# Expert masks of the second token half made inside the FFN block loop, mask and logit copies on ScalarE, and one silu moved ahead of the weight rows

## The chip, the cores and the metric

The kernel runs on one core of one Trainium2 chip. The metric is the device time of one execution in microseconds, the median of the runs. Names used below: TensorE is PE (PEld is its weight load), VectorE is DVE, ScalarE is ACT, GpSimd is POOL, SyncE is SP.

## The reference

Input x has 1024 tokens of 256 features. Four residual stages follow, each with a layer norm in front: attention (16 query heads, 4 key heads, sink and window mask), an FFN with a LoRA mixture of experts, a state-space mixer, and the same FFN with the same weights again. The change touches the FFN only, so it acts twice.

```python
def _L0_ffn_ref(x, gate_w, w_up, w_gate, w_down, up_A, up_B, gate_A, gate_B, down_A, down_B):
    gate_logits = jnp.einsum('bsd,ed->bse', x, gate_w)
    topw, sel = jax.lax.top_k(gate_logits, TOP_K)
    topw = jax.nn.softmax(topw.astype(jnp.float32), axis=1).astype(x.dtype)
    ...
    base_up = xt @ w_up.T
    base_gate = xt @ w_gate.T
    for e in range(NUM_EXPERTS):
        c = jnp.sum(jnp.where(sf == e, wf, 0.0), axis=1)
        lo_up = LORA_ALPHA * (xt @ up_A[e].T @ up_B[e].T)
        lo_gate = LORA_ALPHA * (xt @ gate_A[e].T @ gate_B[e].T)
        h_e = jax.nn.silu(base_up + lo_up) * (base_gate + lo_gate)
        ch = c[:, None] * h_e
        mixed_h = mixed_h + ch
        lora_down = lora_down + LORA_ALPHA * (ch @ down_A[e].T @ down_B[e].T)
    out = mixed_h @ w_down.T + lora_down
```

There are 8 experts of rank 16, so all ranks together are 128 rows. Each token has its top 2 experts. The softmax runs over the tokens (axis 1), so its maximum and sum need the logits of all 1024 tokens.

## The kernel before

All of it is one program written out by hand: for each engine a Python function issues the instructions in the order in which the engine runs them, and semaphores join the engines. `need(e, name, n)` is a wait until counter `name` has reached n. No scheduler moves anything. Float32 products are made of three matmuls of high and low parts (`three`, L167), so most of PE's rows have line 167.

**The FFN** (`ffn`) works on two halves of 512 tokens and on six blocks (`HB`) of 128 hidden features. A unit i = 6h + b is half h, block b, and N = 12. Block 5 holds only 64 features, and its up and gate parts are packed in one bank. The two expert choices of a token are slots 0 and 1. Per unit:

- `base_x(i)`: x times the up and gate weights, 6 matmuls of 512 columns into each of two PSUM banks, `2*which + i % 2` (banks 0 and 2, or 1 and 3). A packed block uses bank `i % 2` alone.
- `base_lora(i)`: adds slot 0's LoRA part from `f_um` (6 matmuls). ScalarE then takes `silu(i, 0)`, and DVE multiplies by the gate, `gated(i, 0)`, which writes `f_t`.
- `second(i)`: adds slot 1's difference to the same banks (6 matmuls), then `silu(i, 1)` and `gated(i, 1)`. It waits for `gated(i, 0)` (counter t0).
- `ch` = `f_t` times the weight row `f_wb`, `mixed` adds both slots, and `hi_parts` (ACT) and `lo_parts` (DVE) split the results in high and low parts. `down(i)` multiplies them (6 matmuls of 512 and 12 of 256 columns).

PE's loop step i runs `base_x(i)`, `base_lora(i)`, `second(i-1)`, `down(i-2)`. `base_x(i)` waits for counter t1 to reach i-1, that is for `gated(i-2, 1)`, which frees the banks. DVE's step i runs `slot(i, 0)` (gated and ch), then `slot(i-1, 1)`, `mixed(i-1)`, `lo_parts(i-1)`. ACT's step i runs `silu(i, 0)`, `silu(i-1, 1)`, `hi_parts(i-1)`.

**Masks.** For each half, `top` finds the best logits of a token, `top_index` their expert numbers, and `one_hot` (L1146) turns these into 0/1 rows `f_hot`. `masks(h)` (L914) transposes them on PE into banks 4 and 5. ACT copies slot 0's mask (`mask0`, L1054), and DVE copies slot 1's and takes the difference (`mask1`, L1160 and L1161). `masked` (L1180) multiplies the LoRA activations `f_us` by the masks in 8 instructions, which write `f_um`. `base_lora` of block 0 waits for the first four of them, `second` for all eight.

**Before the loop** stands the preparation: the layer norm of half 1 (`norm` on DVE, transposes L235 on PE, `hi` on ACT, `lo` L249 on DVE), `logits(1)`, masks of half 0, the softmax's maximum (L975, L978) and sum (L981), `lora_a(1)`, the first units, and `weigh(0)` (L964), which spreads the softmax weights over 128 rows. ACT copies these rows (`weights_out`, L1086). Half 0's layer norm, logits, `lora_a` and `base_x(0)` are issued at the end of the stage in front (`early`). In the first FFN ACT and DVE also split the FFN's weights there (`w_hi` L830, `w_lo` L834). Half 1's index and one-hot rows are made just before and in step 0, its masks in step 2 of PE's loop, and its eight masked products in steps 3 to 5 of DVE's.

## Time and profile before

| | |
|---|---|
| median of 3 runs | 574.26 us (574.2 to 577.9) |
| the profiled execution's own time | 574.69 us |
| its span in the trace | 572.9 us |
| granted TensorE clock | 0.995 |
| PE, DVE, ACT, POOL busy | 523.3, 410.5, 304.3, 131.5 us |

All times of rows are microseconds from the start of the span. The first FFN's preparation lies at 221 to 248 us and its loop from 248 us on; the second FFN's at 445 to 469 us and from 469 us on. A row's idle time and releaser stand in brackets at its end. Rows of several instructions give the time from the first one's start to the last one's end.

### The profile page before, as it was taken

The page shows a single profiled execution, that of the slowest core. Times are in us where ns is not written, and L with a number is a line of the kernel's source. Part 1 is how long each engine was busy: PE and PEld are TensorE (multiplying, and loading weights), DVE is VectorE, ACT ScalarE, POOL GpSimd, SP SyncE. Part 2 cuts the span into 40 slices and gives each one's busy share as a digit, 9 for nine tenths or more (in the row PEclk, how much of TensorE's full clock was granted, in tenths as well). Part 3 has the DMA queues.
Part 4 walks back from the last instruction along what each step waited for, and adds up shares of the span by engine and source line. Part 5 has one row for each costly group of instructions (what it writes and reads, how often), then busy time and mean ns, then how long its engine had stood idle before and what let it go on. Part 6 is the DMA issues. An engine that isn't in the chain of part 4 may idle for free.

```text
span 572.9 us, 9040 instructions
## 1 busy us (share of the span) xinstructions
PE 523.3 (91%) x3031; PEld 439.2 (77%) x3033; DVE 410.5 (72%) x894; ACT 304.3 (53%) x752; POOL 131.5 (23%) x274
## 2 busy tenths in 40 slices
PE   1798899999999979889999999999999889999994
PEld 1577699999999967677887887757778668788884
DVE  6734366666666878889968797966886768886674
ACT  3435677787688643363433454888662245343251
POOL 5511152534342320000000003669443000000000
PEclk9999999999999999999999999999999999999998
DMA  7310010000002103000030000000000000000101
GB/s 269 108 66 1 2 38 0 2 1 2 2 2 72 73 1 133 2 1 0 1 128 2 1 1 1 1 2 1 1 1 2 0 1 1 1 2 0 38 0 38
DMA packets 5790, 14.25 MB, mean 25 GB/s; under 512 B 624, under 2 KB 2928, under 8 KB 5744
## 3 DMA queue, kind: packets, MB, share of 16 engines
q1 hardware_dynamic: 5744, 13.66, 6.8%
q8 instruction: 25, 0.41, 0.3%
q14 instruction: 21, 0.17, 0.1%
HBM read 12.61 MB, written 1.05 MB: 24 GB/s over the span
## 4 chain that ended last, share of the span: by engine, by line
PE 66%; DVE 19%; ACT 6%; issue 6%; POOL 1%; DMA 1%; DVEq 0%; SPq 0%; ACTq 0%; POOLq 0%
PE psum L167 55%; PE psum L446 3%; DVE f_t L1170 2%; DVE f_um L1180 2%; DVE xn L227 2%; PE psum L477 1%; DVE ln_stats L207 1%; DVE oT_hl L665 1%; DMA x_resid<-in_x 1%; PE psum L964 1%; DVE x_resid L672 1%; ACT f_sil L1077 1%; DVE xT_hl L249 1%; ACT qT L540 1%; PE psum L1578 1%
## 5 line engine op out<-in xcount | busy, mean ns | idle before, releaser
L167 PE MATMUL psum<-xT_hl,ffn_w_hl 128*128 128x512 f32 x312 | 78.2, 397 | 7.3 <-DVE f_t L1170 7.3
L167 PE MATMUL psum<-f_um,ffn_w_hl 128*128 128x512 f32 x288 | 72.0, 398 | 1.2 <-DVE f_um L1180 1.2
L167 PEld LDWEIGHTS psum<-xT_hl,ffn_w_hl 128*128 128x128 f32 x312 | 56.3, 188 | 19.6 <-issue 8.7
L167 PEld LDWEIGHTS psum<-f_um,ffn_w_hl 128*128 128x128 f32 x288 | 53.5, 188 | 14.2 <-DVE f_um L1180 2.1
L1170 DVE TENSOR_TENSOR f_t<-psum,f_sil 128x512 f32<-128x512 f32 (+1 forms) x48 | 33.1, 690 | 32.8 <-ACT f_sil L1077 32.2
L1077 ACT ACTIVATE f_sil<-psum 128x512 f32<-128x512 f32 (+1 forms) x48 | 28.2, 595 | 51.9 <-PE psum L167 51.9
L167 PE MATMUL psum<-wo_hl,oT_hl 128*128 128x256 f32 x384 | 50.9, 282 | 4.0 <-DVE oT_hl L665 3.9
L659 DVE TENSOR_TENSOR pT_hl<-psum,pT_hl 126x360 fp32r<-126x360 f32 (+1 forms) x44 | 23.6, 537 | 42.9 <-ACT pT_hl L572 42.9
L167 PE MATMUL psum<-xT_hl,wq_hl 128*128 128x512 f32 x192 | 52.2, 407 | 1.9 <-ACT qT L540 1.9
L167 PEld LDWEIGHTS psum<-wo_hl,oT_hl 128*128 128x128 f32 x384 | 47.7, 188 | 7.5 <-DVE oT_hl L665 5.9
L1098 ACT ACTIVATE f_ch_hl<-f_ch 128x512 fp32r<-128x512 f32 x48 | 30.0, 630 | 41.3 <-DVE f_ch L1227 41.2
L540 ACT ACTIVATE qT<-psum 128x512 f32<-128x512 f32 x32 | 34.9, 1090 | 31.5 <-PE psum L167 31.5
L549 ACT ACTIVATE probs<-probs,small 120x66 f32<-120x66 f32 x120 | 40.5, 344 | 7.8 <-DVE small L642 7.0
L167 PEld LDWEIGHTS psum<-xT_hl,wq_hl 128*128 128x128 f32 x192 | 33.8, 188 | 9.2 <-issue 3.4
L167 PEld LDWEIGHTS psum<-ffn_w_hl,f_mix_hl 128*128 128x128 f32 x288 | 36.9, 188 | 2.8 <-DVE x_resid L1261 0.8
L167 PE MATMUL psum<-f_ch_hl,ffn_w_hl 128*128 128x512 f32 x144 | 37.8, 398 | 1.1 <-DVE f_ch_hl L1239 1.1
L167 PE MATMUL psum<-ffn_w_hl,f_mix_hl 128*128 128x256 f32 x288 | 37.7, 280 | 0.0
L714 POOL TENSOR_TENSOR probs_wide<-probs,small 120x186 f32<-120x186 f32 x40 | 19.9, 498 | 69.7 <-DVE small L622 69.5
L221 POOL TENSOR_TENSOR ln_rstd<-ln_var_eps,minus_half 128x4 f32<-128x4 f32 x8 | 8.3, 1033 | 113.4 <-DVE ln_var_eps L214 113.4
L1227 DVE TENSOR_TENSOR f_ch<-f_t,f_wb 128x512 f32<-128x512 f32 x48 | 33.2, 691 | 1.4
L167 PEld LDWEIGHTS psum<-f_ch_hl,ffn_w_hl 128*128 128x128 f32 x144 | 26.6, 188 | 8.3 <-DVE f_ch_hl L1239 1.7
L167 PE MATMUL psum<-pT_hl,v_hl 126*128 126x360 f32 (+1 forms) x132 | 30.4, 339 | 1.1 <-DVE oT_hl L665 0.6
(238 smaller groups left out, 1129.1 us busy)
## 6 DMA issues: line engine op xcount, KB each, us to landing
w_raw<-in_wq SPq DMA_DIRECT2D x4, 512.0 KB, 3.2
w_raw<-in_wo SPq DMA_DIRECT2D x4, 512.0 KB, 3.3
ffn_w_raw<-in_ffn SPq DMA_DIRECT2D x3, 576.0 KB, 6.1
ffn_w_raw_far<-in_ffn SPq DMA_DIRECT2D x3, 576.0 KB, 6.5
ssd_w_raw<-in_ssd SPq DMA_DIRECT2D x3, 512.0 KB, 5.5
x_resid<-in_x SPq DMA_DIRECT2D x2, 512.0 KB, 4.6
out_x<-x_resid SPq DMA_DIRECT2D x4, 256.0 KB, 2.3
w_raw<-in_wk SPq DMA_DIRECT2D x1, 512.0 KB, 6.7
```

What stands on the lines that cost most here:

```text
L167: i = e.matmul(dst, lhs(a), rhs(b), start=start and n == 0, stop=stop and n == len(TERMS) - 1, **kw)
L227: e.tensor_scalar(xn(t), x[:, t, :], mv[:, t, 0:1], rstd[:, t:t + 1], ALU.subtract, ALU.mult).then_inc(LN["xn"], 1)
L446: m = e.matmul(bank(u % 2)[0:ROWS, i * KBLK:(i + 1) * KBLK], queries_of(q, QB), kw[:, w % W_SLOTS, i, :], start=True, stop=True)
L540: e.activation(qT[:, HALF * half:HALF * half + HALF, h], bank(6), ACT.Copy, scale=float(HD) ** -0.5).then_inc(s_qt, 1)
L549: m = e.activation(p[:, n, :], p[:, n, :], ACT.Exp, bias=NEGM[0:rows, u % 4, n:n + 1], accum_out=DEN[0:rows, u % 4, n:n + 1])
L659: e.tensor_tensor(pT_hl[0:nk, u % 2, LO, 0:n], bank(2 + u % 2)[0:nk, 0:n], f32(pT_hl[0:nk, u % 2, HI, 0:n]), ALU.subtract).then_inc(s_plo, 1)
L714: e.tensor_tensor(wide, p[:, :, SINK:KBLK], spread(r, KB_WIN), ALU.mult)
L1077: e.activation(sil[at_rows, s, :], bank(i % 2)[rows, :], ACT.Silu).then_inc(FS[f"sil{s}"], 1)
L1098: e.activation(ch_hl[:, i % 2, s, HI, :], ch[:, i % 2, s, :], ACT.Copy).then_inc(FS["chh"], 1)
L1170: e.tensor_tensor(tt[rows, s, :], to_bank(i, 1)[rows, :], sil[rows, s, :], ALU.mult).then_inc(FS[f"t{s}"], 1)
L1180: e.tensor_tensor(um_hl[:, h, s, which, w, :], f32(us_hl[:, h, which, w, :]), mT[:, (0, 2)[s], half(h)], ALU.mult).then_inc(FS["um"], 1)
L1227: e.tensor_tensor(ch[:, i % 2, s, :], tt[:, s, :], wb[:, s, half(h)], ALU.mult).then_inc(FS[f"ch{s}"], 1)
```

## The change

- Half 1's masks move from step 2 of PE's loop: slot 0's four transposes stand at the end of step 4 (`MASK_STEP`), slot 1's in step 5 between `base_x(5)` and `base_lora(5)`. Both go to bank 3. Slot 0's wait for t1 = 4, slot 1's for ScalarE's copy of slot 0's mask.
- ScalarE copies all masks out of PSUM (`mask_out`), for half 1 at the end of its step 4, and also the logits of half 1. DVE takes slot 1's difference from the two bf16 copies in SBUF (`mask_diff`).
- On DVE `norm` of half 1 stands ahead of `top_index(0)`. Half 1's `top_index` and `one_hot` move to step 4, its masked products to steps 5 and 6. In half 0 the eighth masked product stands ahead of `gated(0, 0)`.
- On PE the gate part of `base_x(0)` stands behind the transposes of half 1 instead of at the end of the stage in front.
- On ACT `silu(0, 1)` stands ahead of `weights_out(0)`.

```diff
                 else:
                     need(e, "mk0", 1)
-                    need(e, "mk1", 2)
+                    need(e, "mk1", 1)
...
-            def masks(e, h):
-
-                need(e, "ulo", 2 * h + 2)
-                need(e, "hot", 2 * h + 2)
-                for s in range(SLOTS):
-                    for t in range(HT):
-                        m = e.matmul(bank(4 + s)[:, t * P:(t + 1) * P], hot[:, s, HT * h + t, :], identb,
-                                     start=True, stop=True)
-                    m.then_inc(FS["mk"], 1)
+            MASK_BANK = ((4, 5), (3, 3))
+            MASK_STEP = HB - 2
+
+            def masks(e, h, s):
+
+                need(e, "hot", 2 * h + s + 1)
+                if h == 0:
+                    need(e, "ulo", 2)
+                elif s == 0:
+                    need(e, "t1", MASK_STEP)
+                else:
+                    need(e, "mk0", 2)
+                for t in range(HT):
+                    m = e.matmul(bank(MASK_BANK[h][s])[:, t * P:(t + 1) * P], hot[:, s, HT * h + t, :], identb,
+                                 start=True, stop=True)
+                m.then_inc(FS["mk"], 1)
...
                 ln["tr"](e, 1)
+                base_x(e, 0, (1,))
                 base_x(e, 1, (0,))
                 logits(e, 1)
-                masks(e, 0)
+                for s in range(SLOTS):
+                    masks(e, 0, s)
...
                         base_x(e, i)
                         if i == 2:
-                            masks(e, 1)
                             weigh(1)
+                        if i == MASK_STEP + 1:
+                            masks(e, 1, 1)
                         base_lora(e, i)
...
                     if i >= 2:
                         down(i - 2)
+                    if i == MASK_STEP:
+                        masks(e, 1, 0)
...
-                def mask0(h):
-                    need(e, "mk", 2 * h + 1)
-                    e.activation(mT[:, 0, half(h)], bank(4), ACT.Copy).then_inc(FS["mk0"], 1)
+                def mask_out(h):
+                    for s in range(SLOTS):
+                        need(e, "mk", 2 * h + s + 1)
+                        e.activation(mT[:, s, half(h)], bank(MASK_BANK[h][s]), ACT.Copy).then_inc(FS[("mk0", "mk1")[s]], 1)
...
                 ln["hi"](e, 1)
+                need(e, "lg", 2)
+                e.activation(lgT[:, :], bank(6)[0:EXPERTS, :], ACT.Copy).then_inc(FS["lgt"], 1)
                 before["free"](e)
-                mask0(0)
+                mask_out(0)
...
+                silu(0, 1)
                 weights_out(0)
-                silu(0, 1)
...
                         split(4)
-                        mask0(1)
...
                         hi_parts(i - 1)
+                    if i == MASK_STEP:
+                        mask_out(1)
...
-                def mask1(h):
+                def mask_diff(h):
 
                     need(e, "mk0", h + 1)
-                    need(e, "mk", 2 * h + 2)
-                    e.tensor_copy(mT[:, 1, half(h)], bank(5)).then_inc(FS["mk1"], 1)
-                    e.tensor_tensor(mT[:, 2, half(h)], bank(5), mT[:, 0, half(h)], ALU.subtract).then_inc(FS["mk1"], 1)
+                    need(e, "mk1", h + 1)
+                    e.tensor_tensor(mT[:, 2, half(h)], mT[:, 1, half(h)], mT[:, 0, half(h)],
+                                    ALU.subtract).then_inc(FS["mk2"], 1)
...
                 top(e, 0)
+                ln["norm"](e, 1)
                 top_index(e, 0)
-                ln["norm"](e, 1)
...
                 one_hot(0)
-                logits_copy(e, 1)
-                mask1(0)
                 top(e, 1)
...
                 masked(0, 2, 3)
+                mask_diff(0)
...
-                masked(0, 4, 5, 6)
+                masked(0, 4, 5, 6, 7)
                 gated(0, 0)
-                masked(0, 7)
                 split(3)
-                top_index(e, 1)
                 gated(0, 1)
...
                     if i == 0:
                         a_lo(1)
-                        one_hot(1)
+                    if i == MASK_STEP + 1:
+                        masked(1, 0, 1)
                     if i < N and i != 1:
                         slot(i, 0)
-                    if 3 <= i <= 5:
-                        masked(1, *range(3 * (i - 3), min(3 * (i - 2), 8)))
+                    if i == MASK_STEP:
+                        top_index(e, 1)
+                        one_hot(1)
+                    if i == MASK_STEP + 1:
+                        masked(1, 2)
+                    if i == MASK_STEP + 2:
+                        masked(1, 4, 5)
...
-                        if i == 1:
-                            mask1(1)
...
+                    if i == MASK_STEP + 1:
+                        masked(1, 3)
+                        mask_diff(1)
+                    if i == MASK_STEP + 2:
+                        masked(1, 6, 7)
...
-                         lora_a0=lambda e: lora_a(e, 0), base_x0=lambda e: base_x(e, 0),
+                         lora_a0=lambda e: lora_a(e, 0), base_x0=lambda e: base_x(e, 0, (0,)),
```

On PE, in the first FFN's loop from `down(2)` of step 4 to the start of step 6, before (the f_um row is `base_lora(5)` and `second(4)`):

```order
L167 MATMUL psum<-f_ch_hl,ffn_w_hl 128x512 x6
L167 MATMUL psum<-ffn_w_hl,f_mix_hl 128x256 x12
L167 MATMUL psum<-xT_hl,ffn_w_hl 128x512 x6
L167 MATMUL psum<-f_um,ffn_w_hl 128x512 x12
L167 MATMUL psum<-f_ch_hl,ffn_w_hl 128x512 x6
```

The same place now:

```order
L167 MATMUL psum<-f_ch_hl,ffn_w_hl 128x512 x6
L167 MATMUL psum<-ffn_w_hl,f_mix_hl 128x256 x12
L921 MATMUL psum<-const_bf_bits,f_hot 128x128 x4
L167 MATMUL psum<-xT_hl,ffn_w_hl 128x512 x6
L921 MATMUL psum<-const_bf_bits,f_hot 128x128 x4
L167 MATMUL psum<-f_um,ffn_w_hl 128x512 x12
```

Two groups of four mask transposes now stand on both sides of `base_x(5)`; the eight of step 2 (L914) are gone.

On DVE, the first FFN's steps 4 and 5 up to `gated(4, 1)`, before:

```order
L1170 TENSOR_TENSOR f_t<-psum,f_sil 128x512
L1227 TENSOR_TENSOR f_ch<-f_t,f_wb 128x512
L1180 TENSOR_TENSOR f_um<-f_us,f_mT 128x512 x3
L1170 TENSOR_TENSOR f_t<-psum,f_sil 128x512
L1227 TENSOR_TENSOR f_ch<-f_t,f_wb 128x512
L1234 TENSOR_TENSOR f_mix<-f_ch 128x512
L1239 TENSOR_TENSOR f_ch_hl<-f_ch,f_ch_hl 128x512 x2
L1242 TENSOR_TENSOR f_mix_hl<-f_mix,f_mix_hl 128x512
L1170 TENSOR_TENSOR f_t<-psum,f_sil 64x512
L1227 TENSOR_TENSOR f_ch<-f_t,f_wb 128x512
L1180 TENSOR_TENSOR f_um<-f_us,f_mT 128x512 x2
L1170 TENSOR_TENSOR f_t<-psum,f_sil 128x512
```

Now, the part of it that differs, from `ch` of slot 0 in step 4 (first row) and then from the end of `lo_parts(3)` on:

```order
L1241 TENSOR_TENSOR f_ch<-f_t,f_wb 128x512
L890 MAX_INDEX small<-small 128x8 x4
L892 CAST small<-small 128x32
L1161 TENSOR_TENSOR f_hot<-const_bf_bits,small 128x512 x2
L1185 TENSOR_TENSOR f_t<-psum,f_sil 128x512
...
L1256 TENSOR_TENSOR f_mix_hl<-f_mix,f_mix_hl 128x512
L1197 TENSOR_TENSOR f_um<-f_us,f_mT 128x512 x2
L1185 TENSOR_TENSOR f_t<-psum,f_sil 64x512
L1241 TENSOR_TENSOR f_ch<-f_t,f_wb 128x512
L1197 TENSOR_TENSOR f_um<-f_us,f_mT 128x512
L1185 TENSOR_TENSOR f_t<-psum,f_sil 128x512
```

In step 4 the index and one-hot rows stand where three masked products stood; in step 5 two masked products have come ahead of `gated(5, 0)`.

On ACT, the first FFN from the last `f_us` copy of the preparation to loop step 1, before:

```order
L1049 ACTIVATE f_us<-psum 128x512
L1077 ACTIVATE f_sil<-psum 128x512
L1086 ACTIVATE f_wb<-psum 128x512 x2
L1077 ACTIVATE f_sil<-psum 128x512 x2
L830 ACTIVATE ffn_w_hl<-ffn_w_raw_far 128x1152
L1054 ACTIVATE f_mT<-psum 128x512
```

And now:

```order
L1060 ACTIVATE f_us<-psum 128x512
L1091 ACTIVATE f_sil<-psum 128x512 x2
L1100 ACTIVATE f_wb<-psum 128x512 x2
L1091 ACTIVATE f_sil<-psum 128x512
L830 ACTIVATE ffn_w_hl<-ffn_w_raw_far 128x1152
```

`silu(0, 1)` has come ahead of the two weight rows, and the mask copy of step 1 is gone.

## Rows read from the trace of the kernel before

**Rows 1.** The page: busy time, share and instructions of each engine
```profile
PE 523.3 (91%) x3031; PEld 439.2 (77%) x3033; DVE 410.5 (72%) x894; ACT 304.3 (53%) x752; POOL 131.5 (23%) x274
```

**Rows 2.** Busy time by stretch: stretch, length, then busy us (instructions) of each engine
```profile
500.00:560.00 60.00, 60.00 (x311) 50.22 (x309) 44.92 (x70) 23.35 (x39) 0.00 (x0) 1.00 0.03 10
```

**Rows 3.** Timeline, PE in the second FFN's preparation: start, length, engine, line, operation
```profile
448.30 1.03 PE L235 MATMUL psum<-const_f,xn 128*128 128x128 f32 x8
449.09 1.64 PE L167 MATMUL psum<-xT_hl,ffn_w_hl 128*128 128x512 f32 x6
451.34 1.67 PE L167 MATMUL psum<-xT_hl,router_w_hl 128*128 128x512 f32 x6 [0.61 <-DVE xT_hl L249]
...
453.79 0.41 PE L870 MATMUL psum<-const_f,f_lgT 8*128 8x8 f32 x4
...
456.41 0.27 PE L975 MATMUL psum<-const_f,softmax_small 128*2 128x128 f32 x1 [0.62 <-DVE softmax_small L884]
...
460.01 3.04 PE L167 MATMUL psum<-f_um,ffn_w_hl 128*128 128x512 f32 x12
...
463.66 1.67 PE L167 MATMUL psum<-f_um,ffn_w_hl 128*128 128x512 f32 x6 [0.61 <-DVE f_um L1180]
...
469.11 3.01 PE L167 MATMUL psum<-xT_hl,ffn_w_hl 128*128 128x512 f32 x12 [1.99 <-DVE f_t L1170]
```

**Rows 4.** Timeline, DVE and ACT in the same stretch
```profile
446.95 1.38 DVE L227 TENSOR_SCALAR xn<-x_resid,ln_mean_var,ln_rstd 128x256 f32<-128x256 f32 x4
...
453.05 0.68 DVE L864 COPY f_lgT<-psum 8x512 f32<-8x512 f32 x1
453.72 0.60 ACT L1054 ACTIVATE f_mT<-psum 128x512 bf16<-128x512 f32 x1 [3.26 <-PE psum L914]
...
458.55 1.28 DVE L1180 TENSOR_TENSOR f_um<-f_us,f_mT 128x512 fp32r<-128x512 f32 x2
...
460.18 0.17 DVE L1207 RECIPROCAL softmax_small<-psum 128x2 f32<-128x2 f32 x1 [0.35 <-PE psum L981]
...
467.65 1.08 ACT L1077 ACTIVATE f_sil<-psum 128x512 f32<-128x512 f32 x2
468.27 0.69 DVE L1170 TENSOR_TENSOR f_t<-psum,f_sil 128x512 f32<-128x512 f32 x1 [3.89 <-ACT f_sil L1077]
```

**Rows 5.** Timeline, the first FFN: its layer norm, and PE where it waits in the loop
```profile
223.05 1.01 POOL L221 TENSOR_TENSOR ln_rstd<-ln_var_eps,minus_half 128x4 f32<-128x4 f32 x1 [14.11 <-DVE ln_var_eps L214]
...
224.24 1.38 DVE L227 TENSOR_SCALAR xn<-x_resid,ln_mean_var,ln_rstd 128x256 f32<-128x256 f32 x4
225.53 1.35 DVE L834 TENSOR_TENSOR ffn_w_hl<-ffn_w_raw,ffn_w_hl 128x1152 fp32r<-128x1152 f32 x1
...
229.79 1.65 PE L167 MATMUL psum<-xT_hl,router_w_hl 128*128 128x512 f32 x6 [0.63 <-DVE xT_hl L249]
...
247.57 2.97 PE L167 MATMUL psum<-xT_hl,ffn_w_hl 128*128 128x512 f32 x12 [1.99 <-DVE f_t L1170]
...
259.36 2.98 PE L167 MATMUL psum<-xT_hl,ffn_w_hl 128*128 128x512 f32 x12 [0.77 <-DVE f_t L1170]
```

**Rows 6.** Timeline, the second FFN's loop steps 4 and 5
```profile
488.94 2.98 PE L167 MATMUL psum<-xT_hl,ffn_w_hl 128*128 128x512 f32 x12 [0.43 <-DVE f_t L1170]
...
491.76 2.96 PE L167 MATMUL psum<-f_um,ffn_w_hl 128*128 128x512 f32 x12
...
495.33 1.89 DVE L1180 TENSOR_TENSOR f_um<-f_us,f_mT 128x512 fp32r<-128x512 f32 x3
...
497.96 1.63 PE L167 MATMUL psum<-xT_hl,ffn_w_hl 128*128 128x512 f32 x6 [0.44 <-DVE f_t L1170]
...
499.36 0.63 ACT L1102 ACTIVATE f_mix_hl<-f_mix 128x512 fp32r<-128x512 f32 x1
```

**Rows 7.** Groups of DVE instructions by shape: count, busy us and mean ns
```profile
L1146 DVE TENSOR_TENSOR f_hot<-const_bf_bits,small 128x512 bf16<-128x512 bf16 x8 | 5.1, 682 | 0.0
...
L394 DVE CAST xg_hl<-xT_hl 128x1098 fp32r<-128x1098 f32 x2 | 1.6, 791 | 0.0
```

More of the change, by code:

```diff
@@ L765, in build @@
         F_EVENTS = dict(lg=2, lgt=2, lgr=2, lgc=2, m8=NT, ix=NT, ixf=2, hot=4, mt=1, mtT=1, gm=1, dg=1, nm=1, nmc=1, ex=SLOTS, sum=1,
-                        rs=1, wt=1, wb=4, wbc=4, u=4, uhi=4, ulo=4, mk=4, mk0=2, mk1=4, um=16,
+                        rs=1, wt=1, wb=4, wbc=4, u=4, uhi=4, ulo=4, mk=4, mk0=2, mk1=2, mk2=2, um=16,
                         da=2, dd0=4, dd=2, dh=2, dl=2, y=2, add=4)
@@ L990, in down @@
                         need(e, "wbc", 4)
-                        need(e, "mk0", 2)
-                        need(e, "mk1", 4)
+                        need(e, "ulo", 4)
                     if h == 1 and b == 0:
@@ L1173, in masked @@
                 def masked(h, *parts):
-                    if parts[0] == 0:
-                        need(e, "ulo", 2 * h + 2)
-                        need(e, "mk1", 2 * h + 2)
                     for n in parts:
                         s, which, w = n // 4, n // 2 % 2, n % 2
+                        if n == 0:
+                            need(e, "ulo", 2 * h + 2)
+                            need(e, "mk0", h + 1)
+                        if n == 4:
+                            need(e, "mk2", h + 1)
                         e.tensor_tensor(um_hl[:, h, s, which, w, :], f32(us_hl[:, h, which, w, :]),
```

## The prediction

> **What bounds the kernel now.** I read the page's totals first: PE is busy for 523.3 of 572.9 us, DVE for 410.5 [rows 1]. Then the busy time by stretch: in the second FFN's late loop PE is busy for all of 60 us, DVE for 44.9 [rows 2]. So there a faster DVE or ACT is worth nothing, and only PE's idle time elsewhere can be won. Last I read the timeline of both FFN preparations and first loop steps, row by row, for PE's gaps and what ended them. In the second FFN PE waits for the layer norm's low parts (0.61), for the maximum of the logits (0.62), for the last masked product (0.61), and 1.99 for `gated(0, 1)` ahead of `base_x(2)` [rows 3]; then 0.43 and 0.44 at steps 4 and 5 [rows 6]. The first FFN has the same waits and one more of 0.77 at step 3 [rows 5].
>
> I count from start to start, because the bracket begins where the last matmul ends. Twelve matmuls of 512 columns take 2.97 with the last one 0.40 long, so one follows the other after 0.234; six are 1.40, twelve 2.81. Down's twelve of 256 columns take another 1.40. A full step is 2.81 + 2.81 + 1.40 + 1.40 = 8.42; from 488.94 to 497.96 it was 9.02, so the 0.44 wait is worth 0.59. On DVE an instruction of 512 columns lasts 0.68 but the next starts after 0.605 (1.89 for three), or after 0.72 if it needs the result.
>
> **The change, part by part.** Times are those of the second FFN; the first is given where it differs.
>
> A. *Layer norm and order on PE.* `norm` started at 446.95, behind `top_index(0)` [rows 4]. The index takes 0.77 (four searches and a cast), so it starts at 446.18. PE has only half of `base_x(0)` in front and is free in time; the last transposes follow the last tile, at 447.60, and `base_x(0)`'s gate part and `base_x(1)`'s up part, 2.81, bring PE from 447.80 to 450.61. DVE, with the index, one `f_us` part and two low parts behind the norm, is done at 450.15. So the logits start at 450.61 instead of 451.34: 0.73 won, and PE no longer waits there. In the first FFN `norm` can't start ahead of POOL's rstd, which ends at 224.06 [rows 5], and a weight split of 1.27 stands behind it: 224.10 + 1.30 + 0.77 + 1.27 + 0.64 + 1.29 + 0.05 = 229.42, against 229.79: 0.37 won.
>
> B. *Logit and mask copies on ACT.* The logit copy took DVE 0.68; ACT's copy of 512 columns takes 0.60 [rows 4]. The transposed logits then need no place behind the mask copies: DVE's next instruction is `top(1)`. From logits to the transposes at 453.79 were 2.45, now 2.38 (1.67 + 0.05 + 0.60 + 0.06). `top(1)` takes 0.8 and now hides under six matmuls, so the 0.62 wait (0.88 by starts) is gone. Together 0.90 won. The two mask copies on ACT end 1 us before `lora_a(1)` needs their banks, and ACT was waiting there (3.26 in its row), so they cost nothing.
>
> C. *Ahead of `second(0)`.* Everything up to `base_lora(0)` (460.01) moves with A and B. Then DVE has one mask difference more, of which 0.42 fits in its old wait for the sum (458.55 + 2 x 0.605 = 459.76, next start 460.18), so 0.19 remains. `gated(0, 0)` now ends last instead of a masked product: it has the same length, but PE started 0.15 behind a row of that kind and 0.06 behind a masked product. Lost: 0.27.
>
> The difference of the masks has no row, since its inputs are now both bf16 in SBUF. From above the one-hot row bounds it (682 ns) [rows 7], from below a small reciprocal at 0.17. I take the one-hot row; at the low end C loses only 0.08 in each FFN, because the sum then holds DVE. The cast of 1098 f32 columns took 791 ns [rows 7], while a weight split of 1152 columns with two inputs took 1.35 us [rows 5], so DVE does have faster forms here. The Trainium skill, "VectorE: DVE Perf Modes", section "The perf-mode tier table (the rule you actually need)", gives two elements per cycle to a `tensor_tensor` on bf16 in SBUF, an estimated 0.27 less for 512 columns; by it the sum below would be 0.4 larger and the time 569.1.
>
> D. *silu(0, 1) ahead of the weight rows.* The row of two silus at 467.65 stood behind two weight-row copies, which wait for `weigh(0)`; its input was ready 2.3 earlier, when `second(0)` ended at 465.33. Now ACT takes it at once, `gated(0, 1)` is done while PE still runs `weigh(0)`, and the 1.99 wait (2.07 by starts) is gone. The weight rows end 0.1 later than they did, and DVE's `ch` behind them had slack. Won: 2.07. If that cover failed, this is the term to lose.
>
> E. *Steps 2 and 3.* The eight mask transposes leave step 2: 0.46 won. In the first FFN the step also stalled for 0.77 (0.92 by starts), with DVE behind mask copies and a weight split; DVE has two instructions and the one-hot rows fewer there, and I find `gated(1, 1)` done 0.4 before PE is free. Won: 1.4 in the first FFN, 0.5 in the second.
>
> F. *Step 3.* The three masked products that held `gated(2, 1)` are gone: the wait of 0.43 ahead of `base_x(4)`, 0.57 by starts, is won in both.
>
> G. *Step 4.* Index and one-hot rows (0.93 + 1.21 = 2.14) stand where 1.80 of masked products stood, so the wait ahead of step 5 grows by 0.34; four transposes add 0.24. Lost: 0.58.
>
> H. *Step 5.* This is a new wait. `masks(1, 1)` needs ACT's copy of slot 0's mask, and that is queued behind `hi_parts(3)`. Against `gated(3, 1)`, which let PE go at 497.96, `f_mix_hl` started 1.40 later [rows 6]. The mask copy starts 0.53 behind that and takes 0.60, PE sees it 0.06 later: 2.59 in all (rounding kept). PE has 0.24 of transposes and 1.40 of `base_x(5)` to fill it: 0.94 idle, and 0.24 for the second four transposes. Behind the waiting matmul stand `base_lora(5)` and everything else, so all of it counts. Lost: 1.18.
>
> I and J. *Block 6's masked products.* The fourth ends behind `lo_parts(4)`, 8.84 after the start of `base_lora(5)`, and PE wants it at 8.42: 0.42 lost. The last ends 10.04 after `base_lora(6)`, wanted at 9.83: 0.21 lost. `gated(5, 1)` between them comes just in time.
>
> The sum, first FFN: 0.37 + 0.90 - 0.27 + 2.07 + 1.4 + 0.57 - 0.58 - 1.18 - 0.63 = 2.65. Second: 0.73 + 0.90 - 0.27 + 2.07 + 0.5 + 0.57 - 0.58 - 1.18 - 0.63 = 2.11. Together 4.8. What follows each FFN is PE's work or waits for it, so it all moves by as much. The profiled execution took 574.69, 0.43 over the median, so I take 4.8 from 574.26: **569.5 us**, 0.8% less.
>
> **The rivals.**
>
> 1. *The new waits shrink further.* G to J depend on DVE's place in steps 4 to 6. If the difference runs fast (0.4 in both FFNs) and I and J are covered by it and by small slack (1.3), the time is 567.8. For it: 0.42 and 0.21 are small sums of many rows. Against: the difference stands behind the fourth product, so it can't help I. Chance 0.2.
>
> 2. *A wait takes D's place in step 2.* With `base_x(2)` 3.4 earlier, `down(0)` needs high and low parts of `mix`, which stand on ACT behind the second weight rows. By my count they are ready 0.9 before PE asks. If ACT's waits cost 1 us more in each FFN, or E's margin of 0.4 fails, the time is 571.5. Chance 0.18.
>
> 3. *Slower: DVE is the bound from step 4 to 7.* Index, one-hot rows, eight products and the difference are 0.93 + 1.21 + 4.84 + 0.61 = 7.6 us on DVE within three steps, which was spread over six. DVE's idle time in the loop is 15.1 of 60, about 2.1 per step or 6.3 in three [rows 2], less than 7.6, and it lies where DVE waits for a silu. I count 2.4 of PE's time lost per FFN (G to J). If all 7.6 lay open it would be 5.2 more, twice: 579.9. If 2.4 more per FFN lie open the gain is gone; from there it is slower. Against: `gated(4, 1)` and `gated(5, 1)` have 0.6 and nothing to spare, so only the last of them can slip. Chance 0.04.
>
> 4. *The reordered silu does nothing*, since `base_x(2)` is held by something the profile attributes wrongly. Then D is lost: 573.6. For a wrong name speaks nothing: ACT's row ends where DVE's begins. Chance 0.04.
>
> **How the numbers follow.** The forecast has 0.54. My range reaches from rival 1 to a little past rival 2: 567.5 to 571.9. A measurement of this kernel can tell about 1% from no change, which is 568.5. Rival 1 and the low edge of the forecast lie below it: 0.27 for faster. Rival 3's upper part gives 0.03 for slower. The rest, 0.70, is within 1%.
>
> **What would show it.** In the changed profile the 1.99 wait is gone from both FFNs, and PE waits about 1.0 for `f_t` at step 5 (0.8 in brackets), about 0.7 in brackets for ACT's `f_mT` behind `base_x(5)`, and 0.2 for `f_um` ahead of `base_lora(6)`. ACT has six more instructions, DVE six fewer. The logits of the second FFN start 0.7 earlier against `base_x(0)`. I am wrong if PE still waits at `base_x(2)`, if a wait of over 0.3 appears at `down(0)` or `base_x(3)`, or if steps 6 and 7 show DVE busy without a gap and PE behind `gated(5, 1)`.

## The result, and the profile after

The changed kernel takes 568.35 us, the median of five executions (568.20 to 571.18); the kernel before, run beside it on the same chip, takes 575.39 (574.20 to 577.90). The ratio is 0.987, 95% interval 0.985 to 0.990: faster by 1.3%. The forecast was 569.5 us with a range of 567.5 to 571.9, so the time lies in the range, 1.1 us under the forecast. Of the three outcomes it is "faster by over 1%", to which 0.27 was given, and not "within 1%", which had 0.70.

Executions of one kernel lie 1.2 to 4.9 us apart here, and of eleven of the kernel before in one comparison seven took 576.96 to 578.39 at a mean granted clock of 0.989 and four 574.52 to 575.40 at 0.992 or 0.993. A median can shift by that alone, so the sizes below are read from stretches of the trace, in which the two profiled executions of the changed kernel agree to 0.03.

The page after, beside [rows 1]: ScalarE has its six more instructions, VectorE six fewer, and PE is busy 0.9 us longer although the kernel is shorter.

```profile
PE 524.2 (92%) x3031; PEld 440.0 (77%) x3033; DVE 406.9 (71%) x888; ACT 308.0 (54%) x758; POOL 131.6 (23%) x274
```

PE in the second FFN's preparation, beside [rows 3] (timeline: start, length, engine, line, operation):

```profile
449.92 1.56 PE L167 MATMUL psum<-xT_hl,router_w_hl 128*128 128x512 f32 x6
...
452.15 0.41 PE L870 MATMUL psum<-const_f,f_lgT 8*128 8x8 f32 x4 [0.21 <-ACT f_lgT L1075]
...
453.99 0.27 PE L984 MATMUL psum<-const_f,softmax_small 128*2 128x128 f32 x1
...
461.24 1.64 PE L167 MATMUL psum<-f_um,ffn_w_hl 128*128 128x512 f32 x6 [0.68 <-DVE f_t L1185]
...
464.42 3.00 PE L167 MATMUL psum<-xT_hl,ffn_w_hl 128*128 128x512 f32 x12
```

The waits of 0.61 ahead of the logits, 0.62 ahead of the maximum's transpose and 1.99 ahead of `base_x(2)` are gone. From the logits to the transpose at L984 it is now 4.07 us (5.07 in [rows 3]), and from there to `base_x(2)` 10.43 (12.70). Two waits are left in front of the loop: a new one of 0.21 for ScalarE's copy of the logits, and the 0.68 ahead of `second(0)`, which waits for the gated tile now and no longer for a masked product.

Why the 1.99 is gone shows on ScalarE and VectorE in the same place, beside [rows 4]. The silu now stands ahead of the weight row, and the tile that frees `base_x(2)` ends at 464.23, while PE is still at `weigh(0)` (462.71 to 464.66):

```profile
462.91 0.60 ACT L1091 ACTIVATE f_sil<-psum 128x512 f32<-128x512 f32 x1 [3.10 <-PE psum L167]
463.54 0.69 DVE L1185 TENSOR_TENSOR f_t<-psum,f_sil 128x512 f32<-128x512 f32 x1 [2.45 <-ACT f_sil L1091]
463.81 0.60 ACT L1100 ACTIVATE f_wb<-psum 128x512 f32<-128x512 f32 x1 [0.29 <-PE psum L971]
```

The new waits of the loop, beside [rows 6] (PE, the same view):

```profile
492.20 0.38 PE L921 MATMUL psum<-const_bf_bits,f_hot 128*128 128x128 bf16 x4 [0.74 <-DVE f_t L1185]
...
494.85 0.38 PE L921 MATMUL psum<-const_bf_bits,f_hot 128*128 128x128 bf16 x4 [0.82 <-ACT f_mT L1066]
...
504.07 3.06 PE L167 MATMUL psum<-f_um,ffn_w_hl 128*128 128x512 f32 x12 [0.44 <-DVE f_um L1197]
...
512.72 3.27 PE L167 MATMUL psum<-f_um,ffn_w_hl 128*128 128x512 f32 x12
```

They are the waits of terms G, H, I and J; half of J lies inside the last row, which is 3.27 long where an undisturbed one is 2.96. The first FFN shows 0.73, 0.85 and 0.41.

What PE has won over the kernel before, from start to start. A begins at `lora_a(0)` of half 0; the later terms follow each other and end at L984, `second(0)`, `base_x(2)`, `base_x(3)`, `base_x(4)`, `base_x(5)`, `base_lora(5)`, `base_lora(6)` and `base_x(8)`:

| term | predicted, first / second FFN | measured |
|---|---|---|
| A, logits earlier | 0.37 / 0.73 | 0.30 / 0.65 |
| B, logits to maximum's transpose | 0.90 / 0.90 | 0.88 / 1.00 |
| C, on to `second(0)` | -0.27 / -0.27 | 0.02 / 0.00 |
| D, `base_x(2)` | 2.07 / 2.07 | 2.28 / 2.27 |
| E, `base_x(3)` | 1.4 / 0.5 | 1.56 / 0.66 |
| F, `base_x(4)` | 0.57 / 0.57 | 0.68 / 0.62 |
| G, step 4 | -0.58 / -0.58 | -0.38 / -0.40 |
| H, step 5 | -1.18 / -1.18 | -1.19 / -1.18 |
| I, `base_lora(6)` | -0.42 / -0.42 | -0.49 / -0.52 |
| J, `second(6)` | -0.21 / -0.21 | -0.61 / -0.63 |
| sum | 2.65 / 2.11 | 3.0 / 2.5 |

That is 5.5 us against 4.8. The profiled execution of the kernel after reaches the first FFN 0.7 us later than that of the kernel before (that of e9, the same kernel, doesn't), and loses 1.5 more between the FFNs, where TensorE's clock fell. Busy time by stretch of the kernel after, the granted clock third from the end:

```profile
500.00:560.00 60.00, 58.45 (x301) 48.28 (x300) 46.11 (x73) 22.27 (x37) 0.00 (x0) 1.00 0.03 10
438.00:442.00 4.00, 4.00 (x16) 3.39 (x15) 1.45 (x6) 0.00 (x0) 1.10 (x2) 0.59 0.00 0
```

At 0.59 of full speed TensorE is for most of that stretch at the lower of its two levels, 1.2 GHz. The router's six matmuls of half 0 stand in it:

```profile
439.09 2.57 PE L167 MATMUL psum<-xT_hl,router_w_hl 128*128 128x512 f32 x6
```

They take 2.57 us there and 1.55 in the profiled execution of the kernel before.

### The profile page after: what moved, and what is told of

Read it like the earlier page. It is cut to its first block, busy times and chain, and to the rows that moved or that the text cites. A ratio compares the mean times of both kernels' runs of the same rounds, so it can differ in the third digit from the quotient of the medians.

```text
span 569.4 us, 9046 instructions
## 1 busy us (share of the span) xinstructions
PE 524.2 (92%) x3031; PEld 440.0 (77%) x3033; DVE 406.9 (71%) x888; ACT 308.0 (54%) x758; POOL 131.6 (23%) x274
## 4 chain that ended last, share of the span: by engine, by line
PE 66%; DVE 19%; ACT 6%; issue 5%; POOL 2%; DMA 1%; DVEq 0%; SPq 0%; ACTq 0%; POOLq 0%
PE psum L167 55%; PE psum L446 3%; DVE xn L227 2%; DVE f_um L1197 2%; DVE f_t L1185 2%; PE psum L477 1%; PE psum L971 1%; DVE ln_stats L207 1%; DMA x_resid<-in_x 1%; DVE oT_hl L665 1%; DVE f_ch L1241 1%; DVE x_resid L672 1%; PE psum L1601 1%; ACT qT L540 1%; DVE f_mix L1248 1%
```

## The experiments

Besides the times I compare two stretches of PE: from the router's matmuls of half 1 to those of the last `lora_down` in the first FFN, and the same in the second. They leave out the start of the kernel, the mixer and the clock's fall ahead of the second FFN.

| kernel | time, us | ratio to before (95%) | first FFN, us | second FFN, us |
|---|---|---|---|---|
| before | 575.39 | | 120.52 | 115.16 |
| after | 568.35 | 0.987 (0.985 to 0.990) | 117.82 | 113.31 |
| e9_after_again | 570.27 | 0.988 (0.985 to 0.991) | 117.79 | 113.32 |
| e1_silu_back | 574.20 | 0.996 (0.995 to 0.998) | 120.03 | 117.12 |
| e2_silu_alone | 569.59 | 0.989 (0.986 to 0.991) | 118.25 | 112.87 |
| e3_masks_step2 | 566.29 | 0.982 (0.980 to 0.984) | 116.84 | 111.80 |
| e4_loop_best | 564.36 | 0.978 (0.975 to 0.981) | 114.76 | 110.28 |
| e5_mask1_late | 567.94 | 0.986 (0.983 to 0.988) | 117.06 | 112.60 |
| e6_index_early | 566.63 | 0.983 (0.980 to 0.985) | 115.97 | 111.47 |
| e7_products_early | 567.38 | 0.985 (0.982 to 0.987) | 116.75 | 112.32 |
| e8_diff_one_rate | 569.33 | 0.988 (0.985 to 0.991) | 117.97 | 113.49 |
| e10_norm_back | 569.67 | 0.989 (0.985 to 0.992) | 117.71 | 113.37 |
| e11_copies_back | 571.40 | 0.990 (0.987 to 0.994) | 118.01 | 113.51 |
| e12_second_split | 562.88 | 0.975 (0.972 to 0.978) | 114.22 | 109.73 |

The medians of the kernel before in the three comparisons of e1 to e12 were 577.05 (e1 to e4), 577.35 (e5, e6, e7, e9) and 577.30 (e8, e10, e11, e12). The kernel after and its repeat are 1.9 us apart in the median and 0.03 in a stretch.

### e1_silu_back: term D undone

```diff
-                silu(0, 1)
                 weights_out(0)
+                silu(0, 1)
```

> The changed kernel with silu(0, 1) put back behind the two weight-row copies. If the silu's place was what PE waited for (my theory), base_x(2) waits 2.0 again (2.07 to 2.28 by starts) in both FFNs: 4.1 to 4.6 us over the changed kernel, 572.4 to 572.9. If the wait was held by something else (rival), the time stays at 568.3.

Measured 574.20, 5.9 over the kernel after. The wait is back in both FFNs; PE in the second, then its stretch:

```profile
467.07 4.38 PE L167 MATMUL psum<-xT_hl,ffn_w_hl 128*128 128x512 f32 x12 [1.99 <-DVE f_t L1185]
```

```profile
466.00:472.00 6.00, 4.93 (x17) 4.10 (x18) 5.56 (x9) 1.95 (x4) 0.00 (x0) 0.72 0.00 0
```

`base_x(2)` starts 2.23 later, counted from the router. The first FFN's stretch is longer by 2.21, the second's by 3.81: the rest, 1.6, is a fall of the clock behind the wait (0.72 granted; twelve matmuls in 4.38 us instead of 3.00). The profiled execution is the longest of the eleven (576.24), and the same wait in this kernel's first FFN and in both FFNs of the kernel before has no fall behind it. So D is confirmed at 2.2 to 2.3 per FFN, and a fall of the clock can come on top of a wait.

### e2_silu_alone: term D by itself

The same two lines exchanged in the kernel before.

```diff
-                weights_out(0)
                 silu(0, 1)
+                weights_out(0)
```

> The kernel before with silu(0, 1) ahead of the weight rows and nothing else. Theory: the 1.99 waits go, 4.1 us less, 570.1. Rival: with base_x(2) 2 us earlier DVE, which still has one-hot rows and mask copies in steps 0 and 1, is late for base_x(3), and half of it is given back: 572.2.

Measured 569.59. The stretches shrink by 2.27 and 2.29, and the waits of steps 3 to 5 stay as in [rows 5] and [rows 6]. D stands alone: two lines give 4.6 of the 5.5 us, and all else in the change is worth 0.9. That is 0.43 of the first FFN's stretch less 0.44 in the second's, where the kernel after is the longer one, and A's 0.30 and 0.65, which lie ahead of the stretches.

### e3_masks_step2: terms E to J undone

Half 1's masks, index, one-hot rows and products go back to steps 0 to 5; the core of it:

```diff
-            MASK_BANK = ((4, 5), (3, 3))
+            MASK_BANK = ((4, 5), (4, 5))
...
                         if i == 2:
+                            masks(e, 1, 0)
+                            masks(e, 1, 1)
                             weigh(1)
...
+                    if 3 <= i <= 5:
+                        masked(1, *range(3 * (i - 3), min(3 * (i - 2), 8)))
```

> The changed kernel with half 1's masks, one-hot rows and masked products back in steps 0 to 5 (ScalarE still copies), so only the preparation's part of the change stands. In the changed kernel's trace PE's lead over before was 3.48 and 3.92 us at base_x(2) and 3.00 and 2.50 us at the end of the two loops. Theory A: the move into the loop costs 0.5 + 1.4 us on balance, and this kernel takes 566.4. Theory B (my prediction's terms E and F): the move pays for itself because without it steps 2 to 5 wait, and this kernel takes 569.0 or more.

Measured 566.29. The stretches are 0.98 and 1.51 shorter than those of the kernel after. So the part of the change that its description speaks of first, the masks in the loop, loses 2.5 us, and theory A holds, though in the first FFN the loss is twice its 0.5. What came back are waits of 0.33 at step 3 (the first FFN alone) and 0.43 and 0.44 at steps 4 and 5. The wait at step 3 was 0.77 before the change and 0.76 in e2. From `base_x(2)` to `base_x(3)` the first FFN takes 11.26 here, 10.23 after and 11.79 before, so 0.5 of term E's 1.56 doesn't come from the masks' move. This kernel differs there in ScalarE's copies, which leave VectorE one instruction of 0.43 us in step 1 where before it had two of 0.69 and 0.68; that this is the cause is read from the rows, not shown by a run of its own.

### e5_mask1_late: term H alone

```diff
                         if i == 2:
                             weigh(1)
-                        if i == MASK_STEP + 1:
-                            masks(e, 1, 1)
...
                         second(i - 1)
+                    if i == MASK_STEP + 1:
+                        masks(e, 1, 1)
```

and ScalarE's copy of slot 1 moves from behind `hi_parts(3)` to behind `silu(4, 1)`.

> The changed kernel with slot 1's mask transposes of half 1 behind second(4) instead of behind base_x(5), and ScalarE's copy of them behind silu(4, 1); nothing else moves. Theory (term H is a wait of the matmul queue for the bank that slot 0's copy still holds, and everything behind it pays): the wait of 0.85 and 0.82 us behind base_x(5) is gone from both FFNs, 0.95 us each by starts, and the time is 1.9 us under the changed kernel: 566.4 us against 568.3. Rival (the wait only hides that VectorE is full from step 4 to 6, so that PE meets it at base_lora(6) instead): the wait of 0.41 and 0.44 us for f_um grows to over 1 us, and the time stays at 567.8 to 568.5.

Measured 567.94; the stretches are 0.76 and 0.71 shorter. The wait for `f_mT` is gone, and the one behind it has grown from 0.44:

```profile
501.29 3.07 PE L167 MATMUL psum<-f_um,ffn_w_hl 128*128 128x512 f32 x12 [0.64 <-DVE f_um L1199]
```

The theory has the larger part, 0.95 less 0.2; the rival's mechanism is there too, at a fifth.

### e6_index_early: term G alone

```diff
                         slot(i, 0)
-                    if i == MASK_STEP:
-                        top_index(e, 1)
-                        one_hot(1)
...
+                    if i == MASK_STEP - 2:
+                        top_index(e, 1)
+                    if i == MASK_STEP - 1:
+                        one_hot(1)
```

> The changed kernel with half 1's index at the end of step 2 and its one-hot rows at the end of step 3 on VectorE, instead of both in step 4 between gated(3, 0) and gated(3, 1). Theory (term G): the wait of 0.73 and 0.74 us ahead of step 5 is gone, 0.85 us each by starts, while the wait for ScalarE's f_mT behind base_x(5) stays at about 0.85, since it is counted from gated(3, 1) on; 1.7 us less: 566.6 us. Rival (steps 2 and 3 have no room, so a wait for f_t comes up at base_x(3) or base_x(4) in its place): a wait of over 0.4 us there and 567.8 to 568.6 us.

Measured 566.63; the stretches are 1.85 and 1.84 shorter, twice the theory's 0.85. The wait for `f_mT`, expected to stay, is gone as well, together with that of step 4. PE's mask matmuls and ScalarE's copies in the second FFN:

```profile
488.04 0.40 PE L921 MATMUL psum<-const_bf_bits,f_hot 128*128 128x128 bf16 x4
...
489.72 0.40 PE L921 MATMUL psum<-const_bf_bits,f_hot 128*128 128x128 bf16 x4
```

```profile
488.30 0.64 ACT L1116 ACTIVATE f_mix_hl<-f_mix 128x512 fp32r<-128x512 f32 x1
488.84 0.58 ACT L1066 ACTIVATE f_mT<-psum 128x512 bf16<-128x512 f32 x1
```

The same copy in the kernel after, whose first mask matmuls start at 492.20:

```profile
494.13 0.58 ACT L1066 ACTIVATE f_mT<-psum 128x512 bf16<-128x512 f32 x1
```

The slot 0 copy starts 0.80 behind its matmuls (1.93 in the kernel after) and ends at 489.42, ahead of the second matmuls at 489.72. I had counted H from the moment at which `gated(3, 1)` releases PE. With index and rows elsewhere, `gated(3, 1)` and all that hangs on it on ScalarE run 2.0 earlier, counted from the router, and PE, which isn't held by it any more, gains only 0.9 of that up to the first mask matmuls. The rest covers the copy. G and H are one cost: 2.1 us of VectorE's work ahead of `gated(3, 1)`, met once by PE and once more through ScalarE.

### e7_products_early: terms I and J alone

```diff
-                        masked(1, 2)
-                    if i == MASK_STEP + 2:
-                        masked(1, 4, 5)
+                        masked(1, 2, 3)
...
-                        masked(1, 3)
                         mask_diff(1)
-                    if i == MASK_STEP + 2:
-                        masked(1, 6, 7)
+                        masked(1, 4, 5, 6, 7)
```

> The changed kernel with the masked products of slot 0 made at the head of step 5 on VectorE together (the third and fourth next to each other) and the four of slot 1 together at the end of that step, behind the mask difference. Theory (term I is the fourth product's place behind lo_parts(4)): the wait of 0.41 and 0.44 us for f_um ahead of base_lora(6) is gone, 0.5 us each, and with the last products one step earlier the 0.3 us inside second(6)'s row (3.27 instead of 2.96) is gone as well: 0.8 us per FFN, 566.7 us. Rival (VectorE pays at gated(4, 1) or at step 6, where the products now stand): a wait of 0.4 us or more for f_t ahead of base_x(6) or of the step behind it, and 567.9 to 568.8 us.

Measured 567.38; the stretches are 1.07 and 0.99 shorter. No wait for `f_um` is left, and nothing took its place at `base_x(6)`. The row of `base_lora(7)` and `second(6)`, 3.27 after, is undisturbed:

```profile
508.38 2.96 PE L167 MATMUL psum<-f_um,ffn_w_hl 128*128 128x512 f32 x12
```

So VectorE had room for the four products one step earlier. The theory holds; it was a little short (0.8 per FFN).

### e8_diff_one_rate: the mask difference in another form

```diff
-                    e.tensor_tensor(mT[:, 2, half(h)], mT[:, 1, half(h)], mT[:, 0, half(h)],
-                                    ALU.subtract).then_inc(FS["mk2"], 1)
+                    e.scalar_tensor_tensor(out=mT[:, 2, half(h)], in0=mT[:, 1, half(h)], scalar=1.0,
+                                           in1=mT[:, 0, half(h)], op0=ALU.mult,
+                                           op1=ALU.subtract).then_inc(FS["mk2"], 1)
```

> The changed kernel with the mask difference as a scalar_tensor_tensor of the same two bf16 tiles (times 1.0, then the subtraction) in place of the tensor_tensor; the same values come out. Theory (the 420 ns of the tensor_tensor are a faster form that this operation doesn't have): its row is 0.68 us instead of 0.42, VectorE's chain up to gated(0, 0) is 0.26 longer in each FFN, and the wait ahead of second(0) grows from 0.67 to about 0.9: 568.8 us against 568.3. Rival (the short time comes from bf16 in SBUF, whatever the operation): its row stays at 0.42 us, all waits and the time stay as they are.

Groups by shape (count, busy us, mean ns) of the kernel after, then of this one:

```profile
L1175 DVE TENSOR_TENSOR f_mT<-f_mT 128x512 bf16<-128x512 bf16 x4 | 1.7, 420 | 0.0
```

```profile
L1175 DVE SCALAR_TENSOR_TENSOR f_mT<-f_mT 128x512 bf16<-128x512 bf16 x4 | 2.7, 685 | 0.0
```

The same two tiles, 420 ns and 685. The wait ahead of `second(0)` grows from 0.67 to 0.85 in the first FFN and the stretches by 0.15 and 0.18. So the theory holds and the rival falls; the loss is under the expected 0.26. The median, 569.33, lies among those of the kernel after and could not have shown this.

### e10_norm_back: the VectorE half of term A undone

```diff
-                ln["norm"](e, 1)
                 top_index(e, 0)
+                ln["norm"](e, 1)
```

> The changed kernel with norm behind top_index(0) again on VectorE; the new order of the base_x parts on the matmul queue stays. Theory (term A comes from VectorE's place of norm, 0.77 us of index): the router's row of half 1 starts 0.6 to 0.77 us later against base_x(0) in the second FFN, 0.3 to 0.77 in the first, and the time is about 1.1 us over the changed kernel: 569.4. Rival (term A comes from the order of the base_x parts alone, which gives the matmul queue work while the transposes end): both FFNs and the time stay, 568.3.

The median, 569.67, tells nothing here. From `lora_a(0)` to the router's matmuls of half 1 the second FFN takes 9.15 us (before 9.08, after 8.43): there A needs norm's place, and the new order of `base_x`'s parts gives nothing by itself. Norm's place without that order was not run. The first FFN is the other way round: 7.74, where before took 8.52 and after 8.22. The order of the parts gives 0.78, and norm's new place takes 0.48 back. VectorE in the first FFN of e9_after_again, then of this kernel:

```profile
224.15 1.38 DVE L227 TENSOR_SCALAR xn<-x_resid,ln_mean_var,ln_rstd 128x256 f32<-128x256 f32 x4 [0.79 <-POOL ln_rstd L221]
```

```profile
222.54 0.09 DVE L890 MATCH_VALUE_LOAD small<-small 128x8 f32 x1
...
223.34 1.38 DVE L227 TENSOR_SCALAR xn<-x_resid,ln_mean_var,ln_rstd 128x256 f32<-128x256 f32 x4
224.63 1.35 DVE L834 TENSOR_TENSOR ffn_w_hl<-ffn_w_raw,ffn_w_hl 128x1152 fp32r<-128x1152 f32 x1
```

With norm first, VectorE stands idle for 0.79 until POOL's rstd comes, and the index (0.77 from start to start) is still to do in front of the weight split. With the index first it fills just that hole. Neither theory holds for both FFNs. A version with norm first in the second FFN alone was not run.

### e11_copies_back: the copies of term B undone

```diff
                 one_hot(0)
+                logits_copy(e, 1)
+                need(e, "mk", 2)
+                e.tensor_copy(mT[:, 1, half(0)], bank(MASK_BANK[0][1])).then_inc(FS["mk1"], 1)
+                mask_diff(0)
                 top(e, 1)
...
                 masked(0, 2, 3)
-                mask_diff(0)
```

and ScalarE leaves out the logits and slot 1 of half 0.

> The changed kernel with the logit copy, slot 1's mask copy of half 0 and the mask difference of half 0 on VectorE ahead of top(1), as before the change; ScalarE copies slot 0's mask alone. Theory (term B is top(1) standing behind the mask copies on VectorE): top(1) starts 0.6 to 0.7 us later, the wait ahead of the softmax maximum's transpose is back at 0.3 to 0.6 us, and, as the products behind it need no difference any more, up to 0.4 of it is regained ahead of second(0): 0.3 to 0.9 us per FFN, 569.5 us. Rival (VectorE's idle time ahead of top(1) hides the copies): no wait there, 568.3 us.

Measured 571.40, but the stretches are only 0.19 and 0.20 longer: 0.11 up to the maximum's transpose and 0.08 up to `second(0)`. No wait comes back at the transpose. VectorE in the second FFN:

```profile
450.78 0.68 DVE L864 COPY f_lgT<-psum 8x512 f32<-8x512 f32 x1 [0.34 <-PE psum L167]
451.39 0.67 DVE L1211 CAST f_mT<-psum 128x512 bf16<-128x512 f32 x1
452.16 0.42 DVE L1173 TENSOR_TENSOR f_mT<-f_mT 128x512 bf16<-128x512 bf16 x1
452.50 0.18 DVE L878 COPY small<-psum 128x32 f32<-128x32 f32 x1
```

The copies fit almost wholly into VectorE's idle time ahead of `top(1)`. Before, the difference in B was another: the cast of slot 1's mask waited 0.62 for ScalarE's copy of slot 0, and that one for masks that PE made 1.90 behind the start of the logits; here PE makes them 1.40 behind. PE and VectorE of the kernel before, in the same place:

```profile
453.24 0.61 PE L914 MATMUL psum<-const_bf_bits,f_hot 128*128 128x128 bf16 x8 [0.22 <-DVE f_hot L1146]
```

```profile
454.35 0.69 DVE L1160 CAST f_mT<-psum 128x512 bf16<-128x512 f32 x1 [0.62 <-ACT f_mT L1054]
```

e11 puts the copies back, but not the order in which the cast stands behind ScalarE's copy. So their lengths, the theory's cause, are worth 0.2 per FFN and not 0.3 to 0.9. That the wait carried the rest is read from these rows; no run here isolates it. It isn't norm's place: e10 has norm back, and from the logits to the maximum's transpose its second FFN takes 4.08 (after 4.07).

### e4_loop_best and e12_second_split: a better placing

e4 joins e5, e6 and e7.

> The changed kernel with four moves: slot 1's masks of half 1 stand behind second(4) and their copy behind silu(4, 1), the index rows stand at the end of step 2, the one-hot rows at the end of step 3, and the masked products with the first four ahead of gated(4, 1), the last four at the end of step 5. Theory: the waits of 0.74, 0.82 and 0.44 and the 0.3 in second(6) go, with the 0.15 behind each that the bracket leaves out: 2.8 us in each FFN, 562.7. Rival: DVE has no room for it and PE waits at base_x(4) to base_x(7) instead: 566 or more.

Measured 564.36; no wait is left in steps 3 to 6, and the stretches are 3.06 and 3.03 shorter than after. e6 and e7 by themselves sum to 2.92 and 2.83, so e5's part, worth 0.7 alone, adds 0.1 to 0.2 beside them: the wait that it removes is the one that e6 removes too. Expected were 562.7 us; the spread of these executions, 561.05 to 565.86, doesn't tell whether the rest is more than that.

e12 adds to e4 the last wait of the preparation:

```diff
                     if b == 0:
-                        need(e, "um", 8 * h + 8)
+                        need(e, "um", 8 * h + 6)
                     need(e, "t0", i + 1)
                     for which in range(2):
+                        if b == 0 and which:
+                            need(e, "um", 8 * h + 8)
...
-                masked(0, 4, 5, 6, 7)
+                masked(0, 4, 5, 6)
                 gated(0, 0)
+                masked(0, 7)
```

> The best version so far (index, one-hot rows, products and slot 1's masks of half 1 placed apart in the loop) with one more change ahead of second(0): gated(0, 0) stands ahead of the last masked product, and the matmul queue waits for six products ahead of second(0)'s up part and for all eight ahead of its gate part. Theory (gated(0, 0) is ready one product earlier, and the last product isn't wanted until six matmuls later): the last wait of the preparation, 0.67 us, falls to about 0.1 and 0.6 us per FFN are won: 563.2 us against 564.4. Rival (gated(0, 0) then waits for its silu, or the last product for PE): the wait stays over 0.5 us, 564.4 us.

Measured 562.88, ratio 0.975 (0.972 to 0.978), the shortest median of all. The stretches are 0.54 and 0.55 shorter than e4's, and the wait is gone, as the theory has it; its two edits were not run apart. In the second FFN PE runs from `base_lora(0)` through `second(0)` without a pause, eighteen matmuls in one row, and VectorE's gated tile stands one product earlier:

```profile
452.08 4.79 PE L167 MATMUL psum<-f_um,ffn_w_hl 128*128 128x512 f32 x18
```

```profile
452.56 1.89 DVE L1201 TENSOR_TENSOR f_um<-f_us,f_mT 128x512 fp32r<-128x512 f32 x3
454.40 0.69 DVE L1189 TENSOR_TENSOR f_t<-psum,f_sil 128x512 f32<-128x512 f32 x1
455.00 0.68 DVE L1201 TENSOR_TENSOR f_um<-f_us,f_mT 128x512 fp32r<-128x512 f32 x1
```

### e9_after_again: the changed kernel once more

> The changed kernel itself, beside its variants, as their common bound. Both theories: 568.3 us, 571 where the clock drops ahead of the second FFN as it did in its profiled execution; ratio to the kernel before 0.987 to 0.990.

Six executions of 567.23 to 571.61, median 570.27, and the same waits to 0.02. In its profiled execution the clock fell in the same place as in that of the kernel after (the router row of half 0 takes 2.52):

```profile
438.34 2.52 PE L167 MATMUL psum<-xT_hl,router_w_hl 128*128 128x512 f32 x6
```

In e7's it didn't:

```profile
436.48 1.55 PE L167 MATMUL psum<-xT_hl,router_w_hl 128*128 128x512 f32 x6
```

## Why the prediction was right, and where it was not

**The size.** The forecast rested on D, and D came: 2.28 and 2.27 against 2.07, and e1 and e2 show it from both sides. The rows place the small surplus. From `weigh(0)` to `base_x(2)` PE took 3.94 from start to start and takes 1.71 now, 2.23 less: the bracket of 1.99 begins where the last matmul ends, and one that isn't held starts 0.24 ahead of that end, of which the prediction counted 0.08. H came to a hundredth of its 1.18, by starts, and the releasers of all three new waits were named right. As the sum, 5.5 against 4.8 is an error of 0.7 in the rows; the rest of the distance to the measured time is the spread of the executions.

**C, sign and size.** The step that took "the one-hot row" (682 ns) for the difference of the masks failed: it takes 420 ns. The one-hot row reads "bf16<-128x512 bf16", but that names its output and its first input alone. Its second input, the expert number, is float32 in the kernel (`idxf`, a view of the F32 tile `small`) and is repeated over 128 columns, so this row was not of the difference's form. Which of the two keeps it at 682 no run separates. e8 shows that with all tiles bf16 the operation decides too. The prediction's low end bounded the difference only by a tiny reciprocal and charged C 0.08 for it; measured is nothing at all, 0.02 and 0.00. With the single rate e8 loses 0.17, less than my 0.27, so the rest of C was rated too dear as well. The Trainium skill, "VectorE: DVE Perf Modes", section "The perf-mode tier table (the rule you actually need)", gives the faster rate to a `tensor_tensor` on bf16 in SBUF; this trace agrees, with 265 ns less than the other operation (the estimate was 270). The rule stood in the prediction and was weighed below the one-hot row. It would have moved the forecast to 569.1.

**E, F.** Right, each 0.05 to 0.16 short. In the second FFN's E no wait was removed. There `weigh(1)`, `base_lora(2)` with `second(1)`, and the first row of `down(0)` take 0.06, 0.05 and 0.07 less from start to start, of which the prediction had almost nothing; the rows don't say why.

**G, H: right in size, wrong as two terms.** G was 0.2 too dear: the index and one-hot rows stand 2.10 long where 2.14 was counted, the transposes cost 0.20 instead of 0.24, and `base_x(4)`, which waits no more, is 0.09 shorter. H was worked out as a chain that starts where `gated(3, 1)` releases PE, and for the kernel as changed that is so. But it was called a new wait of its own, and e6 shows that it belongs to G's cause: with index and rows out of step 4 both are gone (1.85), while removing H's place alone (e5) gives 0.75.

**J.** Predicted 0.21, measured 0.6. Half is in the late product itself (0.31 inside the row), and about 0.1 at each of three restarts of the loop, which I had counted nowhere. e7 gives back 1.0 for I and J together, measured at 1.1; predicted was 0.63.

**A.** The sum was right in both FFNs (0.30 and 0.65 against 0.37 and 0.73), the reason in one only. For the first FFN I had seen that norm can't start ahead of POOL's rstd and wrote the index behind it into the sum; I didn't ask what the index had done in front of it. e10 shows that the change pays 0.48 there.

**B.** The size was right (0.88 and 1.00 against 0.90; the prediction's own two parts, 0.07 and 0.88, add up to 0.95), the cause half: "the transposed logits then need no place behind the mask copies" isn't it, since e11 puts them back for 0.11. The gain is in what the mask copies waited for.

**The rivals.** The first (time 567.8) was the nearest beside the forecast. Its first part is right, the difference ran fast and C's 0.54 for both FFNs went, but its second, slack that covers I and J, is wrong: they were dearer. The second didn't happen: there is no wait at `down(0)` or ahead of `base_x(3)`. The third named VectorE in steps 4 to 7 as the place of the loss, and e6 and e7 agree with the place, at 2.9 us per FFN. It wasn't a lack of VectorE's time, though: with the same instructions placed otherwise (e4) no wait of PE is left in steps 3 to 6. The fourth fell with D.

**The chances.** The two medians differ by 7.0 us and the rows by 5.5; the line between "within 1%" and "faster" was at 5.7. A sum that comes to within 1 us of such a line can't carry 0.70 on one side where executions of one kernel are 3 us apart. That the median lies within 1.1 us of the forecast is in part luck: the rows alone are 0.7 off, and the medians moved by 1.5 more than the rows.

## What to carry to other kernels

Ask first which instruction of an engine's queue stands ahead of the one on the path and was ready later: exchanging two lines of ScalarE gave more than the rest of this change together. When work moves into a loop, spread it: 2 us of index and one-hot rows in the one place ahead of a tile that two engines wait for were paid at two places, 0.9 each, and at neither when they stood at the ends of steps 2 and 3. And where executions differ by more than the effect, compare one stretch of the trace from start to start; it resolved 0.17 us where the medians of one kernel were 1.9 apart. And the type in a row is that of the first input alone: before a row's time is carried over to another instruction, look up its second input in the kernel.

## What the runs showed of the hardware that was not expected

A VectorE `tensor_tensor` of two bf16 tiles in SBUF, 128x512, takes 420 ns; as a `scalar_tensor_tensor` on the same tiles it takes 685, and the one-hot `tensor_tensor`, whose second input is float32 and repeated, 682 [rows 7].

TensorE's clock falls in some executions and not in others of the same instructions. In the profiled executions after and of e9 it fell at the end of the mixer, 1.6 to 1.7 us after PE had gone on behind a wait of 1.03 for `x_resid`; the six router matmuls take 2.57 and 2.52 there. The kernel before, e1, e2, e7 and e8 have the same wait ahead of the same matmuls and take 1.55 or 1.56. e1's clock fell later, behind the 1.99 wait. The falls measured here cost 1.5 and 1.6 us. What decides whether one comes is open.
